# Padding rows of an expert-sorted slot table copied in the last round; weights in eight loads; the table's fills earlier; the last sums in a tile of their own

## What is computed

```python
h = tok_kernel(x, log_dt, B_ri, inv_A_real, A_imag, 512)        # [16, 256, 512]
h = concatenate([broadcast(cls_tok), h], axis=1)                # [16, 257, 512]
h = h + attn(layernorm(h), ...)    # gates = u @ W_in; scan over t; y @ W_out + x @ W_skip
x = layernorm(h).reshape(-1, 512)                               # 4112 rows
scores = softmax(x @ gate_w)                                    # 8 experts
topk_w, topk_idx = top_k(scores, 2)
routed = sum over the 2 chosen e: topk_w * (silu(x @ w_gate[e]) * (x @ w_up[e])) @ w_down[e]
shared = silu(x @ sw_gate) * (x @ sw_up) @ sw_down
out = h + routed + shared
```

## Time and profile before

| | us |
|---|---|
| median of 3 runs | 1201.91 (1198.83 to 1205.6) |
| the profiled execution | 1199.16 |
| its span, first to last instruction | 1197.5 |
| TensorE busy | 1067.0 (89%) |
| VectorE busy | 812.8 (68%) |
| ScalarE busy | 347.0 (29%) |
| GpSimd busy | 381.0 (32%) |
| mean granted TensorE clock | 0.953 of full |
| moved by DMA | 191.97 MB, 160 GB/s over the span |

### The profile page before, as it was taken

The page is one execution under the profiler, slowest core; times in us unless marked ns, Lnnn a source line. Parts: engine busy times, 40 slices in busy tenths (PEclk is TensorE's granted clock), DMA queues, the critical chain, the costliest instruction groups (busy, mean ns, idle before and its releaser), DMA issues.

```text
span 1197.5 us, 26578 instructions
## 1 busy us (share of the span) xinstructions
PE 1067.0 (89%) x7943; PEld 697.0 (58%) x7944; DVE 812.8 (68%) x2123; ACT 347.0 (29%) x658; POOL 381.0 (32%) x352
## 2 busy tenths in 40 slices
PE   3087848999999999999999869889999999999994
PEld 3055625677766776677766635655555555555552
DVE  7976939888998889988899366444444444444442
ACT  4313413433444334443444133111111111111110
POOL 1010211221232212321122021135555556555564
PEclk8588977999999999999999979899999999999998
DMA  8323494655455554555545877579999777878774
GB/s 261 96 54 84 127 332 111 160 172 162 124 155 176 165 161 115 161 177 155 146 131 172 323 215 263 182 154 202 194 174 198 130 133 127 132 131 130 132 124 71
DMA packets 309167, 191.97 MB, mean 160 GB/s; under 512 B 258082, under 2 KB 276898, under 8 KB 306932
## 3 DMA queue, kind: packets, MB, share of 16 engines
q1 hardware_dynamic: 292500, 144.22, 47.7%
q0 software_dynamic: 15504, 36.46, 15.0%
q10 hardware_dynamic: 1104, 10.54, 2.2%
HBM read 59.69 MB, written 88.12 MB: 123 GB/s over the span
## 4 chain that ended last, share of the span: by engine, by line
PE 75%; DMA 5%; DVE 3%; issue 2%; SPq 2%; ACT 1%; POOLq 0%; POOL 0%; ACTq 0%; DVEq 0%
PE bank L999 28%; PE bank L1169 11%; PE bank L1159 11%; PE bank L1160 10%; PE bank L1074 8%; PE bank L1013 4%; DMA mixed<-h_tok 2%; DMA out<-x2w,rows_in 1%; SPq L877 1%; DMA h_tok<-tokens 1%; DMA x_slots<-x3w,sl 1%; PE bank L1078 1%; PE bank L1064 1%; SPq L816 1%; DMA wexp<-x3w 1%
## 5 line engine op out<-in xcount | busy, mean ns | idle before, releaser
L999 PE MATMUL bank<-wexp 128*128 128x256 f16 (+2 forms) x3252 | 410.4, 287 | 43.7 <-DVE h L1553 34.9
L999 PEld LDWEIGHTS bank<-wexp 128*128 128x128 f16 x3252 | 310.7, 99 | 127.3 <-DVE h L1553 35.6
L1159 PE MATMUL bank<-wexp,rows_in 128*128 x852 | 255.5, 313 | 8.0 <-issue 6.1
L1160 PE MATMUL bank<-wexp,rows_in 128*128 x852 | 255.1, 312 | 0.0
L929 POOL TENSOR_TENSOR inv<-var,power 128x4 f32<-128x4 f32 x17 | 29.2, 1716 | 398.4 <-DVE var L1545 398.4
L977 POOL DMA_INDIRECT out<-x2w,rows_in x71 | 113.3, 1596 | 114.7 <-DMA out<-x2w,rows_in 77.5
L1701 DVE SCALAR_TENSOR_TENSOR mixed<-bank,mixed 128x352 f32<-128x352 f32 x71 | 37.2, 524 | 159.8 <-ACT mixed L1320 157.6
L965 POOL TENSOR_TENSOR ex<-base,ld 128x8 f32<-128x8 f32 x71 | 118.8, 1674 | 77.0 <-DVE ld L1680 57.3
L1159 PEld LDWEIGHTS bank<-wexp,rows_in 128*128 128x128 f16 x852 | 83.0, 97 | 65.3 <-issue 25.1
L1320 ACT ACTIVATE mixed<-bank 128x352 f32<-128x352 f32 x71 | 32.9, 464 | 293.9 <-PE bank L1160 288.6
L1169 PE MATMUL bank<-wexp,gates 128*128 (+1 forms) x477 | 111.7, 379 | 2.6 <-DVE x2w L1696 2.6
(11 more groups left out here) (283 smaller groups left out, 1268.8 us busy)
## 6 DMA issues: line engine op xcount, KB each, us to landing
w_halves<-rows_in SPq DMA_DIRECT2D x16, 704.0 KB, 4.8
wexp<-w_halves ACTq DMA_DIRECT2D x1, 8704.0 KB, 27.3
wexp<-w_halves SPq DMA_DIRECT2D x8, 1088.0 KB, 6.2
h_tok<-tokens SPq DMA_DIRECT2D x16, 512.0 KB, 2.7
mixed<-h_tok SPq DMA_DIRECT2D x32, 256.0 KB
pads<-zrow SPq DMA_DIRECT2D x4, 2048.0 KB, 16.9
out<-h SPq DMA_DIRECT2D x32, 256.0 KB
w_halves<-rows_in SPq DMA_DIRECT2D x16, 384.0 KB, 5.0
```

The lines of the kernel that those rows point to most:

```text
L999: last = MM(dst, stat_of(step, a), mov_of(step, b), start=(s_ == 0 and a + b == 0), stop=(s_ == len(steps) - 1 and a == 1))
L1159: MM(GB[:, 0:H], xT[b][:, a, c, :], wexp[:, u, o:o + H], start=s_, stop=e_)
L1160: last = MM(UB[:, 0:H], xT[b][:, a, c, :], wexp[:, u, o + H:o + 2 * H], start=s_, stop=e_)
```

## The change

 The padding table has two rows of 128 for each expert in place of four; its zero part is filled by one transfer in round -1 and one in round 0, behind the token load, in place of four in round 1. room is called in the last round, behind the last chunk's place, and pad_rows copies 128 rows in place of 384; SyncE issues five copies ahead of the first loads of the expert stage and waits for all eight there, ScalarE issues three between its silus, and GpSimd's scatter waits for none. The first eight units of weights are loaded by eight DMAs at four places of rounds 15 and 16. The last tile's sums go to h2, which is free by then, without the wait for an earlier add.

```diff
-    pads_d = nc.dram_tensor("pads", [E, 4, P, XW], F16).ap()
+    pads_d = nc.dram_tensor("pads", [E, 2, P, XW], F16).ap()
...
+        sums_of = lambda i, b: h2[:, 0, 0, :] if isinstance(i, int) and i == NSLOT - 1 else yo[b % 2][:]
...
-            row = eng.value_load(runi[0:1, e:e + 1], min_val=0, max_val=ZERO - 3 * P)
-            eng.dma_start(xs_d[bass.ds(row, 3 * P), :], pads_d[e].rearrange("r q w -> (r q) w")[bass.ds(turn, 3 * P), :]).then_inc(c_z, 16)
+            row = eng.value_load(runi[0:1, e:e + 1], min_val=0, max_val=ZERO - P)
+            eng.dma_start(xs_d[bass.ds(row, P), :], pads_d[e].rearrange("r q w -> (r q) w")[bass.ds(turn, P), :]).then_inc(c_z, 16)
...
@@ SyncE, body(k, q), behind the token load
+                    if isinstance(k, int) and k in (-1, 0):
+                        for r in range(k + 1, k + 2):
+                            sp.dma_start(pads_d[:, r, :, 0:2 * D]..., zrow...broadcast_to([P, E, D])).then_inc(c_pw, 16)
...
-                    if isinstance(k, int) and k == NCH:
+                    if isinstance(k, int) and k == LAST:
                         sp.wait_ge(c_ri, 1)
-                        sp.wait_ge(c_pw, 128)
-                        for e in range(4):
+                        sp.wait_ge(c_pw, 64)
+                        for e in range(5):
                             pad_rows(sp, e)
-                    if isinstance(k, int) and k == LAST:
                         sp.wait_ge(c_wo, 32 * NCH)
+                        sp.wait_ge(c_z, 16 * E)
                         sp.wait_ge(c_sca, 64 * (NCH + 1))
                         sp.wait_ge(d_tb, 1)
                         for b in range(4):
                             load(b, b)
...
-                            if i == 1 and isinstance(k, int) and k == NCH:
-                                pad_rows(sp, 4)
...
-                    if isinstance(k, int) and k == NCH:
-                        pad_rows(sp, 5)
...
-                    if isinstance(k, int) and k == 1:
-                        for r in range(4):
-                            sp.dma_start(pads_d[:, r, :, 0:2 * D]..., zrow...).then_inc(c_pw, 16)
                     if isinstance(k, int) and k == 2:
                         sp.wait_ge(c_pd, 1)
-                        for r in range(4):
+                        for r in range(2):
...
@@ SyncE and TensorE, ahead of the expert stage
+                sp.wait_ge(d_w0, 16 * (E - 1))
                 sp.wait_ge(d_w, 16)
...
+                pe.wait_ge(d_w0, 16 * (E - 1))
                 pe.wait_ge(d_w, 16)
...
@@ GpSimd, ahead of the scatter
-                        if isinstance(k, int) and k == LAST:
-                            gp.wait_ge(c_z, 16 * E)
...
-                                                 in_=yo[b % 2][:], in_offset=None, compute_op=ALU.add).then_inc(d_ys[b % 2], 16)
+                                                 in_=sums_of(i, b), in_offset=None, compute_op=ALU.add).then_inc(d_ys[b % 2], 16)
...
@@ ScalarE, body(k, q)
-                    if isinstance(k, int) and k == NCH - 1:
-                        act.wait_ge(c_tokm, NCH * 2)
-                        act.wait_ge(c_wo, 32 * E)
-                        act.dma_start(wexp[:, 0:E, :], w16_d[0:E].rearrange("u p n -> p u n")).then_inc(d_w, 16)
+                    def first_weights(u):
+                        if isinstance(k, int) and k in (NCH - 1, NCH):
+                            if k == NCH - 1 and u == 0:
+                                act.wait_ge(c_tokm, NCH * 2)
+                                act.wait_ge(c_wo, 32 * E)
+                            u += 4 * (k - NCH + 1)
+                            act.dma_start(wexp[:, u, :], w16_d[u]).then_inc(d_w if u == E - 1 else d_w0, 16)
                     if has(k - 1):
                         silu(k - 1, 0)
+                    first_weights(0)
...
                         silu(n, 1)
                         ghigh(n, 0)
+                        if isinstance(k, int) and k == LAST:
+                            act.wait_ge(c_ri, 1)
+                            act.wait_ge(c_pw, 64)
+                            pad_rows(act, 5)
                         silu(n, 2)
+                        if isinstance(k, int) and k == LAST:
+                            pad_rows(act, 6)
                         ghigh(n, 1)
+                        first_weights(1)
                         silu(n, 3)
+                        if isinstance(k, int) and k == LAST:
+                            pad_rows(act, 7)
                         ghigh(n, 2)
...
                         ghigh(n, 4)
+                        first_weights(2)
                         ghigh(n, 5)
-                    if isinstance(k, int) and k == NCH:
-                        act.wait_ge(c_ri, 1)
-                        act.wait_ge(c_pw, 128)
-                        pad_rows(act, 6)
                     if has(k):
                         rows_hi(k, 0, q)
-                    if isinstance(k, int) and k == NCH:
-                        pad_rows(act, 7)
...
                         rows_hi(k, 1, q)
+                    first_weights(3)
...
@@ VectorE, body(k, q): room() behind place(k - 1) of the last round, no more of round 16
                         if at_last:
                             place(k - 1)
+                            room()
...
                             place(k - 1)
-                            room()
...
@@ VectorE, out_of(i, b)
-                    at_least(v, d_ys[b % 2], halfcount(i, b) - 16)
-                    TS(yo[b % 2][:], DB[:], wv[:, b % 2:b % 2 + 1], 1.0 / SW, ALU.mult, ALU.mult).then_inc(d_ye, 1)
+                    if not (isinstance(i, int) and i == NSLOT - 1):
+                        at_least(v, d_ys[b % 2], halfcount(i, b) - 16)
+                    TS(sums_of(i, b), DB[:], wv[:, b % 2:b % 2 + 1], 1.0 / SW, ALU.mult, ALU.mult).then_inc(d_ye, 1)
```

More of the change, by code:

```diff
@@ L727, in vit_tower @@
         d_w = sem("d_w")
+        d_w0 = sem("d_w0")
         d_tb = sem("d_tb")
```

4 lines of the change are left out of this document (2 added, 2 removed).

## The result

The changed kernel takes 1169.34 us (median, 1167.34 to 1172.73) against 1202.09 us (1198.83 to 1205.6) for the kernel before: ratio 0.973, interval 0.9694 to 0.9766. The prediction was 1161 us with a range of 1153 to 1171. So it is 32.75 us faster where 41 were forecast from the median shown. The profiled execution took 1168.93 us (span 1167.2); before it was 1199.16 (span 1197.5), a difference in span of 30.3 us, to be compared with the forecast sum of 38.7.

The account below looks back on a forecast made before the run. TensorE's own work was taken as the bound, leaving only its holes to win back: 21.2 + 15.6 + 4 - 4 + 1.9 = 38.7 us off the profiled execution gives 1160.5, stated as 1161 us, range 1153 to 1171.

Parts of the forecast that it names:

- the milder rivals: Three rivals of 1169 to 1170 us: weight pieces hold token load (0.14), dearer copies (0.10), early fills delay first rounds (0.05).
- Part 1: Rounds 2 and 3: zero fills moved off the token load's queue end VectorE's 19.1 us wait; gain 21.2 us, bounds 17 to 27.1.
- the 2.1 us added for the clock: Head of round 3: 96 products return from 12.71 to 10.65 us once the hole of round 2 is gone.
- Part 2: Round 15: weights in eight transfers let the token load land earlier, closing TensorE's 14.8 us hole; gain 15.6 us, bounds 10 to 16.5.
- The rival that the pieces still hold the load: Round 15: load catches two transfers, TensorE idles 7 us, transposes before round 17 meet the last unit; 1170 us, chance 0.14.
- The alternation by packets: Skill rule: engines alternate between queue rows packet by packet, so the token load's small packets still wait behind large weight packets.
- Part 3: Before round 17: padding copies removed from round 16 shorten TensorE's wait for transposes and its clock loss; gain 4 us, bounds 1 to 8.9.
- Part 4: Round 17: row loads wait for eight copies landed there, first expert product at 781.3 instead of 777.35; loss 4 us, bounds 0 to 12.
- The rival of dearer copies: Round 17: copies land late or ScalarE's copies delay the shared part in series; loss 12 instead of 4, 1169 us, chance 0.10.
- Part 5: Kernel's end: last sums go to a free tile without waiting for an earlier add; gain 1.9 us, bounds 0 to 4.4.
- slower: Round 17: eight copies run one after another before the first load; loss 53.5 instead of 4, 1210 us, chance 0.03.
- no effect: All three holes: VectorE or the clock takes back what the transfers give; chance 0.01.

Follow-up runs that it names:

- the last two versions: Changed kernel with the last weight unit in round 17 and filler products in TensorE's holes, the second also spreading copies over SyncE, ScalarE, GpSimd: 1161.06 and 1161.01 us.

## Why the prediction was right, and where its terms were off

The sign, the places of the gains and of the new wait, and the order of the parts held, and 1169.34 is in the range. It is so only by its upper edge: the forecast's own bounds were 1153 to 1168, and the last 3 us were added for the milder rivals, none of which came true as a whole. Each part stayed inside its own bounds, but the large misses went the same way. The sum was 8.4 us too good (38.7 against 30.3 in the profiles), 3.3 of it in part 1 and 4.9 in part 4. What the two have in common is clock lost behind short holes, which the prediction priced behind the long ones only.

- **Part 1** (21.2 forecast, 17.9 measured). Right: the load of round 2 issued at 146.87 where 147.0 was said, statistics at 153.42 where 153.45 was said, no hole in rounds 0 and 1. The step that failed is the 2.1 us added for the clock, and with it the claim that rounds 2 and 3 come out at 42 and 38. The prediction named the seats and seated work of VectorE as what TensorE would wait for, and gave it no price: two holes of 1.90 and 1.58 us, features of 6.46 us instead of 3.79, and 13.15 us for the 96 products, which is worse than before. The short holes kept the clock loss that the long one had: against a round of 38.09 us, rounds 2 and 3 are 9.1 us too long, 3.5 of it these two holes and 5.2 slow products.
- **Part 2** (15.6, measured 15.4 in round 15). The load was waited for 1.40 us, where the forecast implied 3.4 to 6.4 (data at 678.0 or 681, VectorE there at 674.6), and TensorE idled nowhere in the round on VectorE, only 1.19 us at its end on a transpose. The rival that the pieces still hold the load is excluded there; its second half, that the last unit meets the transposes before round 17, is true, for 2.2 us in round 16. The alternation by packets that was weighed against this change did not show itself as a cost: the first unit left at 651.03 and had landed after 5.2 us, the load beside it left at 653.24 and was read at 658.45, 5.2 us later, no more than the 5.4 of an undisturbed one.
- **Part 3** (4, measured 2.6 in round 16). The idle time came out as said: 4 us were kept, partly for the last unit that goes out before the second transpose, and 3.62 stand there; moving that unit showed 2.2 us to be its share. The gain in idle time is 2.5 us, not 2.9, since the 6.9 us of before held 0.8 us of router products. The term that was mis-sized is the clock: of the 2.0 us lost in the 24 products half was to go, and it grew by 0.6 instead (5.28 against 4.66 us), which stands in round 17's column. The part was also costed alone, when it is not: with the weights in eight and the copies left in round 16 that round took 11.1 us more.
- **Part 4** (-4, measured -8.9). The first load came 743.22 - 728.79 = 14.4 us after room where some 14 was said. That is in part luck: the five copies were issued in 8.86 us where 9.4 were counted, and a copy landed in 4.3 us where 2.5 were taken. Round 17 was 29.58 us where 781.3 - 753.2 = 28.1 was worked out: 0.6 of the slow products at its head and 0.9 because the load needed 747.26 - 743.22 = 4.0 us instead of 3.1. The step that failed is what was left out: the hole before the experts was taken as its length, without the clock behind it and behind the next one, 3.1 of the 3.5 us in the first tiles. The rival of dearer copies (-12) had the direction of the miss right (8.9 lies between 4 and 12) and its cause wrong: copies on SyncE landed in 4.3 us and didn't hold each other.
- **Part 5** (1.9, measured 2.5 in the tail of two profiles). The medians show no difference when it is undone, and the tails of equal code spread by 1.3 us, so the term is neither confirmed nor refuted. The 2.1 us that it took from the sums to the add stayed (2.18 us).
- The rivals slower and no effect fell: eight copies were issued in 14.94 us by one engine and did not wait for each other's landing.

What stays open: why a hole of about 2.6 us costs the clock in one execution and not in another; what TensorE waits for before the third tile (2.47 us after, 2.39 and 2.51 in the last two versions), since the profile names no releaser there (with all copies on SyncE the same hole, 2.02 us, is put down to VectorE's mixed); and what part 5 is worth.

## What to carry to other kernels

Price a hole at its length and the slower products that may follow it, also for the small holes that remain when a large one closes. When a big transfer is cut in pieces, look at each piece for what it stands beside and not only for who needs it: one piece of 1.09 MB held the transposes beside it by 2 us here. Parts that share the DMA engines are to be costed together, since undoing one of them with the other in place gave a time that neither cost alone would give. Before a profile is said to show what an edit did, look at the same stretch in the profiles of other kernels that have the same code there.

## What was not expected of the hardware

- Nearly the same hole, 2.57 us in one kernel and 2.66 in another, was followed by a granted clock of 0.68 over the 5 us from 745 on (the first products at 1.2 GHz, then 2.4) in the first and 1.00 in the second.
- A copy of 264 KB with its place read from a register costs the issuing engine 2.06 us on SyncE, and 1.8 us from one to the next on GpSimd (731.49 to 733.27), so eight of them are bound by issue and not by the 2.1 MB that they move.
- With copies of 6.3 MB and units of 1.09 MB under way, an indirect scatter of GpSimd landed 14.9 us after its issue, and the transposes after 6.2 and 7.7 us.
- Equal code differs by up to 5 us between executions in two places: up to the start of round 2 (140.23 to 144.99 us in the kernels with one fill each in rounds -1 and 0) and between the first and the last down product (389.2 to 394.3 us). No run shows why, and it is as much as most of the medians differ by.
